# Cross attention on TensorE: score and value products put between projection products, in place of one kind after the other

## The reference, cut to what matters

```python
q = x @ Wq
kv = context @ Wkv
k, v = jnp.split(kv, 2, axis=-1)
sim = jnp.einsum('bhid,bhjd->bhij', q, k) * SCALE
sim = jnp.where(mask[:, None, None, :], sim, max_neg)
sim = jnp.clip(sim, -5.0, 5.0)
attn = jax.nn.softmax(sim, axis=-1)
out = jnp.einsum('bhij,bhjd->bhid', attn, v)
```

## Time and profile before

| | us |
|---|---|
| median of 3 runs | 3541.45 |
| lowest, highest | 3529.15, 3542.26 |
| the profiled execution's own time | 3545.98 |
| its span, first to last instruction | 3544.2 |
| TensorE matmul busy in the span | 3312.9 |
| VectorE, ScalarE, GpSimd busy | 1815.3, 1482.1, 1628.8 |

### The profile page before, as it was taken

The page is one execution under the profiler, slowest core; times in us unless marked ns, Lnnn a source line. Parts: engine busy times, 40 slices in busy tenths (PEclk is TensorE's granted clock), DMA queues, the critical chain, the costliest instruction groups (busy, mean ns, idle before and its releaser), DMA issues. The chain is left out here.

```text
span 3544.2 us, 52758 instructions
## 1 busy us (share of the span) xinstructions
PE 3312.9 (93%) x19140; PEld 2842.0 (80%) x19140; DVE 1815.3 (51%) x2937; ACT 1482.1 (42%) x2749; POOL 1628.8 (46%) x1118
## 2 busy tenths in 40 slices
PE   6999999999999999999999996889999787799997
PEld 4888888888888888888888885767767565678897
DVE  4454554555555455455555556575674634532213
ACT  3455555555555555555555542153453405221000
POOL 4454555455555455455555544041441316246573
PEclk9999999999999999999999998899999989899998
DMA  5211110111111111011101105100000120124221
GB/s 198 72 38 36 45 45 25 46 45 45 38 34 46 36 45 42 29 45 46 44 28 44 38 2 148 37 27 26 2 3 1 52 74 1 47 68 124 78 85 37
DMA packets 116365, 170.32 MB, mean 48 GB/s; under 512 B 12144, under 2 KB 89328, under 8 KB 107376
## 3 DMA queue, kind: packets, MB, share of 16 engines
q1 hardware_dynamic: 113264, 158.23, 14.2%
q0 software_dynamic: 2816, 8.46, 0.7%
HBM read 143.52 MB, written 23.13 MB: 47 GB/s over the span
## 5 line engine op out<-in xcount | busy, mean ns | idle before, releaser
L427 POOL TENSOR_TENSOR es<-es,e 128x512 f32<-128x512 f32 x480 | 622.7, 1297 | 966.1 <-ACT e L493 965.8
L489 ACT ACTIVATE e_hl<-sc 128x512 fp32r<-128x512 f32 x512 | 323.7, 632 | 738.7 <-DVE sc L557 738.4
L585 PE MATMUL ps_p<-c_hi,wkv_lo 128*128 128x512 f32 x1024 | 402.9, 393 | 4.6 <-PEq L115 4.6
L585 PE MATMUL ps_p<-c_lo,wkv_hi 128*128 128x512 f32 x1024 | 402.5, 393 | 0.0
L585 PE MATMUL ps_p<-wkv_lo,c_hi 128*128 128x512 f32 x1024 | 401.6, 392 | 0.0
L585 PE MATMUL ps_p<-wkv_hi,c_lo 128*128 128x512 f32 x1024 | 401.5, 392 | 0.0
L515 DVE TENSOR_TENSOR k_lo<-ps_p,k_hi 128x512 fp32r<-128x512 f32 x256 | 175.7, 686 | 440.6 <-ACT k_hi L455 440.6
L585 PE MATMUL ps_p<-c_hi,wkv_hi 128*128 128x512 f32 x1024 | 399.4, 390 | 0.0
L585 PE MATMUL ps_p<-wkv_hi,c_hi 128*128 128x512 f32 x1024 | 398.3, 389 | 0.0
L515 DVE TENSOR_TENSOR v_hl<-ps_p,v_hl 128x512 fp32r<-128x512 f32 x256 | 177.1, 692 | 429.4 <-ACT v_hl L455 428.4
L557 DVE TENSOR_SCALAR sc<-ps_s,topi 128x512 f32<-128x512 f32 x512 | 379.7, 742 | 0.3 <-PE ps_s L635 0.2
(11 more groups left out here) (401 smaller groups left out, 7083.7 us busy)
## 6 DMA issues: line engine op xcount, KB each, us to landing
raw<-in_ctx_t SPq DMA_DIRECT2D x64, 1024.0 KB, 4.9
dense_raw<-in_L_ffn_W_experts SPq DMA_DIRECT2D x64, 256.0 KB, 2.9
raw<-in_L_xattn_Wkv SPq DMA_DIRECT2D x4, 1024.0 KB, 4.8
q_hi_scratch<-qa_qh SPq DMA_DIRECT2D x16, 256.0 KB, 2.5
q_lo_scratch<-qa_ql SPq DMA_DIRECT2D x16, 256.0 KB, 3.4
q_hi<-q_hi_scratch SPq DMA_DIRECT2D x32, 128.0 KB, 5.0
q_lo<-q_lo_scratch SPq DMA_DIRECT2D x32, 128.0 KB, 4.7
o_t_scratch<-o_sb SPq DMA_DIRECT2D x32, 128.0 KB, 2.3
```

Of the source, the lines that this page charges most:

```text
L427: g.tensor_tensor(ES[:, GL], ES[:, GL], e, ALU.add).then_inc(summed, 1)
L489: a.activation(E2[:, s % 2, :, 0, :], sc, ACT.Exp, scale=DH ** -0.5).then_inc(exp_hi, 1)
L585: mm = t.matmul(ps_p[:, par % 2, :], lhs, rhs, start=m == 0, stop=m == 3 * KC - 1)
```

## The change

The order in which TensorE issues its matmuls in a slot. Scores and values keep their order among themselves, and so do the unit's matmuls; the number of matmuls, their operands, their sizes and the semaphores that they raise stay as they are. In a slot with a unit the 6 scores and the first 6 products of the unit take turns, then come the wait for the exponentials and the values, and then the 4 values take turns with products 7 to 10, and products 11 and 12 follow. The waits for `clo_done` and for `p_free` ahead of the unit move to the head of the slot. All other engines' programs are unchanged.

```diff
+            def product(kind, n, hf, cb, par, m):
+
+                k, part = divmod(m, 3)
+                w, c = ((W_lo, C_hi), (W_hi, C_lo), (W_hi, C_hi))[part]
...
+                mm = t.matmul(ps_p[:, par % 2, :], lhs, rhs, start=m == 0, stop=m == 3 * KC - 1, skip_group_check=True)
+                if m == 3 * KC - 1:
+                    mm.then_inc(proj_done, 1)
+
             def project(kind, n, hf, cb, par):
...
+                for m in range(3 * KC):
+                    product(kind, n, hf, cb, par, m)
+
+            def score(s, m):
+
+                hf, blk, GL, kt = place(s)
+                pr, n = divmod(m, 3)
+                k_, q_ = ((K_lo, Q_hi), (K_hi, Q_lo), (K_hi, Q_hi))[n]
+                mm = t.matmul(ps_s[:, s % 2, pr * 256:(pr + 1) * 256], k_[:, 2 * GL + pr, kt * P:(kt + 1) * P], q_[:, hf, 2 * GL + pr, :],
+                              start=n == 0, stop=n == 2, skip_group_check=True)
+                if m == 5:
+                    mm.then_inc(scored, 1)
+
+            def value(s, j):
...
+                if j == GRP - 1:
+                    mm.then_inc(pv_done, 1)
+
+            def values_ready(s, i, S, first):
 
                 hf, blk, GL, kt = place(s)
                 t.wait_ge(e_lo, S + 1)
...
-                    for pr in range(2):
-                        c = 2 * GL + pr
-                        for n, (k_, q_) in enumerate(((K_lo, Q_hi), (K_hi, Q_lo), (K_hi, Q_hi))):
-                            mm = t.matmul(ps_s[:, s % 2, pr * 256:(pr + 1) * 256], k_[:, c, kt * P:(kt + 1) * P],
-                                          q_[:, hf, c, :], start=n == 0, stop=n == 2)
-                    mm.then_inc(scored, 1)
-                    if not (first and s < LAG):
-                        values(s - LAG, i - (s < LAG), S - LAG, first)
-                    if has_kv(s, last):
+                    unit = has_kv(s, last)
+                    if unit:
                         kind, n, of, cb = unit_of(s)
                         if s % BS == KT and not (first and s < BS):
 
                             t.wait_ge(clo_done, KC * (i * SLB + s // BS))
                         t.wait_ge(p_free, unit_at(i, s) - 1)
-                        project(kind, n, of, cb, unit_at(i, s))
+                    for m in range(6):
+                        score(s, m)
+                        if unit:
+                            product(kind, n, of, cb, unit_at(i, s), m)
+                    late = not (first and s < LAG)
+                    if late:
+                        values_ready(s - LAG, i - (s < LAG), S - LAG, first)
+                    for m in range(6):
+                        if late and m < GRP:
+                            value(s - LAG, m)
+                        if unit:
+                            product(kind, n, of, cb, unit_at(i, s), 6 + m)
```

More of the change, by code:

```diff
@@ L574, in _ @@
         def _(t):
-            def project(kind, n, hf, cb, par):
[L577 to L587, removed]
@@ L589, in values @@
-            def values(s, i, S, first):
+            def product(kind, n, hf, cb, par, m):
+                k, part = divmod(m, 3)
+                w, c = ((W_lo, C_hi), (W_hi, C_lo), (W_hi, C_hi))[part]
+                if kind == K:
+                    lhs, rhs = w[:, k, (HP * hf + n) * P:(HP * hf + n + 1) * P], c[:, cb, k, :]
+                else:
+                    lhs, rhs = c[:, cb, k, n * P:(n + 1) * P], w[:, k, INNER + hf * 512:INNER + (hf + 1) * 512]
+                mm = t.matmul(ps_p[:, par % 2, :], lhs, rhs, start=m == 0, stop=m == 3 * KC - 1, skip_group_check=True)
+                if m == 3 * KC - 1:
+                    mm.then_inc(proj_done, 1)
@@ new lines, in value @@
+            def value(s, j):
+                hf, blk, GL, kt = place(s)
+                mm = t.matmul(ps_o[:, 2 * GL + j // 2, (j % 2) * 256:(j % 2 + 1) * 256], V2[:, kt, GRP * GL + j, :],
+                              E2[:, s % 2, j].rearrange("p e q -> p (e q)"),
+                              start=(blk == 0 and kt == 0 and j % 2 == 0), stop=(blk == M // BLK - 1 and kt == KT - 1),
+                              skip_group_check=True)
+                if j == GRP - 1:
+                    mm.then_inc(pv_done, 1)
@@ L594, in values @@
                     t.wait_ge(rec_done, 4 * i + 2 * hf + GL - 1)
[L595 to L600, removed]
             def total(i, n):
@@ L653, in _ @@
             for s in range(SL - LAG, SL):
-                values(s, B - 1, SL * (B - 1) + s, False)
+                values_ready(s, B - 1, SL * (B - 1) + s, False)
+                for j in range(GRP):
+                    value(s, j)
             total(B, -1)
```

## The result

| | before | after |
|---|---|---|
| median, us | 3537.62 (5 runs, 3529.15 to 3542.26) | 3558.04 (5 runs, 3557.6 to 3562.38) |
| profiled execution, us | 3545.98 | 3562.38 |
| its span, us | 3544.2 | 3560.6 |

The changed kernel takes 1.007 times as long, 95% interval 1.0054 to 1.0085, clear of noise; the medians lie 20.4 us apart, which is 1.0058. A second time, with other runs of the kernel before, the ratio was 1.007 again (1.0053 to 1.0087). Two of the 29 runs of the kernel before on that chip, 5041.85 and 7416.99 us, were slow ones and don't count in any ratio. The forecast was 3532 us and no measurable change. The time lies inside the range given, on the side that had a chance of 0.19.

What follows compares the result with a forecast made beforehand. TensorE's matmul stream without holes was taken to bound cross attention. Gaps summed to -13 us, taken as -10, and waits to 0; from 3541.45 us that gave about 3532 us, range 3486 to 3578.

Steps and rivals of the forecast that it cites:

- What bounds it: In cross attention TensorE runs matmuls without holes at granted clock 1.00; the gap between two matmul starts decides.
- The first and second of "three things": Gaps in a slot: narrow behind wide 0.113 us, wide behind narrow 0.232; slot 3.914 against 3.94, -13 us, taken as -10.
- rival C: Wide gaps in a slot never settle: 0.236 us, narrow 0.120; +46 us and +4 of waits, 3591 us; chance 20%.
- rival A: Matmul gaps in a slot stay flat, price and discount of a boundary cancelling; 3532 us; chance 47%.
- Rival B: Gaps in a slot shrink for narrow and wide matmuls, to 0.113 and 0.2257 us; -50 us, 3491; chance 29%.
- The third, PSUM banks at nothing: Neighbouring matmuls in a slot now write to different PSUM banks; costed at nothing.
- The loads: TensorE's weight loads each start with the matmul before their own, so one load lies beside one matmul; no averaging.
- rival D: Weight loads run further ahead of the matmuls; at best 159 us less, 3382 us; chance 4%.
- The chain moves by 0.5 us: Later scores delay VectorE's clip and the ScalarE and GpSimd work behind it by 0.5 us, not 1.1.
- The batch starts: At seven batch boundaries the later chain becomes a TensorE wait, 3.5 us at most, 2 expected; vanishing e_hl waits cancel it.

Runs made afterwards that it cites:

- the streams: Matmuls by themselves, each with its own weight load, nothing of the model computed; narrow and wide in turn took 0.3467 or 0.3533 us a pair.
- The four buffers: The changed kernel with four buffers for the exponentials in place of two; 3548.69 us, 1.0039 times the kernel before.
- late values and four buffers: The kernel before with its four values, still together, put behind the unit's tenth product, and four buffers for the exponentials in place of two; ratio 0.9987.

## Why the prediction was wrong

- **What bounds it: right.** TensorE stays the bound at a granted clock of 1.00; after, it is busy 298.68 of 300.00 us from 1200 to 1500. TensorE doesn't wait in ordinary slots; its waits are at group ends and batch starts.
- **The first and second of "three things", the failed term.** They gave a pair 0.345 us. Measured over the stretch it is 0.116 + 0.233 = 0.349, against 0.348 for the kernel before. The sum said -13 us and I took -10; it is +9.1. The 0.113 and the 0.232 were read rightly; what failed is putting them together as the steady price of a pair, when in the rows each had been read at one boundary with a long block on either side. Taking turns has a state of its own, in one slot of three 0.354. In the other two the pair takes 0.347, and the slots of 3.92 are the forecast's 3.914 but for 8 ns: if all slots had been like them, 18 ns below the 3.94 of before, that would have been 9 us less, as forecast. In the slots of 4.01 the gaps of 0.12 and 0.24 stand that were named as the sign of rival C. Nor do price and discount cancel at a boundary, the premise of rival A. The price falls on five wide ones (28 ns together above 0.2267), the discount on one narrow one (7 ns), which agrees with the 20 ns of the streams. Rival C named the direction but not the state: it had the narrow gap at 0.120 throughout and a cost of 46 us. Rival B's short narrow gap came true in part, its wide one of 0.2257 did not.
- **The third, PSUM banks at nothing: right.** One bank or two made no difference in the streams.
- **The loads: right.** After, too, each load starts with the matmul before its own (913.48, 913.60 and 913.84 in both timelines), and rival D is out. (At 0.325 us a pair the slot of rival D comes to 3.68 us, not 3.69; nothing hangs on it.)
- **"The chain moves by 0.5 us", the second failed term.** I followed the scores to the clip and left out the wait of line 487. It stands on the values, which the change puts 2 us later. The exponential moved by 1.4 us and es_lo by 1.26. With that, a wait that the forecast gave no term at all, `total` for es_lo, became 14 us. Its row before, 3.0 us once, was in the view that I read. The four buffers take back 10 of the 14 us. With them the chain moves by 0.64 us and the clip starts 2.06 into the slot (2.34 without them), so for the scores alone 0.5 and 2.0 were nearly right; but `total` had only half a microsecond of room, and the waits that remain come of that.
- **The batch starts: right in place, about right in size.** The waits on v_hl are 0.8 us of matmuls and 2.8 of loads, where 2 were forecast; those on e_hl fell from 1.3 to 0.5 and did not quite go. They do cancel about.

The two failures have the same sign and, less the 1 us that the waits at other places fell, add up to the 22.2 us of the stretch. That the time lies in the range is luck of its width: the range took in rival C for another reason and at more than twice the cost.

What chooses between the two modes of a stream in turn stays open. The stream at 0.3467 follows a pause (its first matmul starts 1.24 us after the one before it), those at 0.3534 follow a matmul without one; that wasn't tried by itself. And a pause isn't needed: in the kernel, and in the stream of its order, two wide ones at the end of a slot are enough to go from one mode to the other.

The order with late values and four buffers is a little below the kernel before, 0.9987 (0.9975 to 0.9998); that is barely more than nothing.

## What to carry to other kernels

When instructions of one engine are reordered, list every semaphore that each moved one raises, and ask of each waiter when it now gets it; a write into a buffer that a moved instruction reads is such a waiter, and here it cost 11 us, as much as the order was forecast to gain. A row of waits that is small now still names a wait that can grow, so ask how much room it has. A price that is read at one boundary between two blocks isn't the price of a stream made of boundaries. A stream of the same shapes by itself gave each slot length of the kernel to 1 ns, so an order is cheap to try before it is built in.

## What was not expected of the hardware

- The gap of a matmul depends on several matmuls before it. Behind a block of narrow ones five wide ones take 0.233, 0.236, 0.228, 0.233 and 0.231 us before 0.2267 holds, with all other engines idle, and in the kernel.
- One stream in turn, two lasting modes: 0.3467 and 0.3534 us a pair. One shape by itself has more than one steady gap too, at a granted clock of 1.00: 512 wide 0.2267 us in the streams and 0.2337 in the dense block, 256 wide 0.120 and 0.113. Why stays open.
- The Trainium skill, "TensorE: Matmul & The Clock Gate", in the section on the back-to-back issue gap, gives N/2.4 + 2.5 ns for an isolated warm gap. With a load per matmul these runs show 0.120 us for 256 columns and 0.2267 for 512, 10.8 and 10.9 ns above it.
